# Softmax maxima of an attention stage turned by the DMA engines through DRAM, in place of TensorE and ScalarE

## The chip, the cores and the metric

The kernel runs on one core of one Trainium2 chip. The metric is the device time of one execution in microseconds. Before the change the median of three runs is 2610.9 us (2610.55 to 2611.96).

## The reference

A gated layer for 8 batches: `x` and `ctx` are 8 x 512 x 1024 (channels by positions). It normalizes `x` over its last axis, attends to `ctx` with 16 heads of 32 channels, adds the result times a gate, normalizes again, and adds a product with a 1024 x 1024 matrix whose operands are rounded to 8-bit floats, again gated.

```python
q = Wq @ layernorm(x) + bq; k = Wk @ ctx + bk; v = Wv @ ctx + bv      # per batch, 16 heads of 32 rows
dot  = einsum('bhdt,bhds->bhts', q, k) / sqrt(32)
mask = target_mask[:, :, :, None] * source_mask[:, :, None, :]
dot  = mask * dot - (1.0 - mask) * 1e6
amap = softmax(dot, axis=-1) * mask
x = x + tanh(g_xattn) * einsum('bhts,bhds->bhdt', amap, v)
x = x + tanh(g_ffn) * (f8(scale * layernorm(x)) / scale) @ (f8(scale1 * W2) / scale1)
```

## The kernel before

There are three stages. Setup turns the weights. The projections (to about 570 us) write q, k and v to DRAM scratch. The attention stage is where the change lies.

It works through 32 quads, a quad being four heads of one batch, in periods of 64 slots. TensorE issues all work in one written order (`period(n, p)` of the tensor block). In slot k of period n it issues one score matmul of quad n (`scores`, line 690): keys on the partitions, 512 queries in the columns, slots 0 to 31 for the query half th=0 and 32 to 63 for th=1. Beside it stands one matmul of the same scores the other way round, queries on the partitions (`scores_for_max`, line 703), 19 slots ahead of the quad's own period by `XLEAD` and `maxima_at`. VectorE takes each one's maximum along the row (line 849). Every fourth slot P·V follows (`times_v`, line 716), every eighth the sums of the probabilities (`denominators`, line 727), and at slots 34, 35, 50 and 51 the last product for quad n - 2 (`ffn`, line 742).

The softmax needs the maximum subtracted, and the score matmul does it: its operands have 100 rows, 96 for the products and two for the mask, and rows 98 and 99 of the stacked queries `q_st` hold the negated maximum of each query, in two parts (`KX, KS = 98, 100`). The maxima come out of VectorE with queries on the partitions, as `neg_max`, 128 x 32. They must become two rows of 16 x 128. Before the change that is done so: at slots 23 (th=1 of quad n) and 55 (th=0 of quad n+1) TensorE turns `neg_max` by a matmul with the identity (`turn_max`, line 734) into one of the three `x_bank` banks, ScalarE copies it out (`copy_max`, line 803), and SP writes it to `q_st` by one DMA (`set_max`, line 1035). `scores` waits for that DMA at slots 0 and 32 (`max_set`).

VectorE negates at slots 19 and 51 (`negate_max`, lines 858 to 865). The table `JOBS` deals the three banks to maxima, ffn halves and the two turns in order; `freed` says what each user waits for.

SP issues nearly all DMAs of the stage in one written order, and a wait of one holds all behind it. Around the two places: `turn_y8` (line 1031, a DMA transpose), `move_inv` (1011) and `spread_inv` (1017), which carry the inverse sums to DRAM and back for GpSimd's multiplication (line 951), `load_tm`, `load_v`, `move_den` (1007), the store of the output (`store`, 1044), and at the start of a period `stack` (990 to 996), the next quad's operands.

## Time and profile before

| | |
|---|---|
| median of 3 runs | 2610.9 us |
| the profiled execution's own time | 2608.16 us |
| its span | 2606.3 us |
| TensorE busy | 2505.3 us, 96% |
| VectorE busy | 1978.2 us, 76% |
| GpSimd busy | 1653.4 us, 63% |
| ScalarE busy | 1393.0 us, 53% |
| DMA | 242040 packets, 314.48 MB |
| matmuls of line 734 (the turn) | 64, median 298 ns |
| copies of line 803 | 64, median 266 ns |

The engine shares are over the whole span. The attention stage is a row of equal periods of some 61 us, so one period, cut out by windows and read in a timeline, stands for 30 others. Where a time is given without "us after", it is microseconds from the span's start.

### The profile page before, as it was taken

The numbers are of one execution on the slowest core, as the hardware profiler recorded it, in microseconds if no ns is written. First come the engines' busy times: TensorE is split into PE (matmuls) and PEld (weight loads), VectorE is DVE, ScalarE is ACT, GpSimd is POOL, SyncE is SP. The second block draws the span as 40 slices with busy tenths as digits, with TensorE's granted clock in tenths as the row PEclk, the third lists the DMA queues.
The fourth block names the chain that finished last, engine by engine and source line by source line (L and its number), as shares of the span: only waits on it lengthen the run. The fifth ranks groups of instructions, "written<-read, shape, count | busy, mean of one in ns | idle before, by whom it ended". The sixth has DMA issues, their size and how long they took to land.

```text
span 2606.3 us, 40566 instructions
## 1 busy us (share of the span) xinstructions
PE 2505.3 (96%) x13169; PEld 1385.0 (53%) x13169; DVE 1978.2 (76%) x3251; ACT 1393.0 (53%) x2606; POOL 1653.4 (63%) x1265
## 2 busy tenths in 40 slices
PE   5999999978999999999999999999999999999995
PEld 4888888864444444444444444444444444444441
DVE  5766666637788888888888888888888888888863
ACT  2333333322666666666666666666666666666662
POOL 1333333422777777777777777777777777777774
PEclk8999999996999999999999999999999999999997
DMA  6666666655334444444444444344444444444411
GB/s 213 229 236 236 234 234 233 237 171 96 76 80 89 88 96 91 98 103 99 103 98 93 91 93 93 88 88 88 96 91 96 102 100 102 100 94 92 91 37 49
DMA packets 242040, 314.48 MB, mean 121 GB/s; under 512 B 75033, under 2 KB 142681, under 8 KB 241857
## 3 DMA queue, kind: packets, MB, share of 16 engines
q1 hardware_dynamic: 229712, 274.20, 42.2%
q10 hardware_dynamic: 12144, 38.02, 4.1%
q8 instruction: 93, 1.52, 0.3%
q14 instruction: 91, 0.74, 0.1%
HBM read 200.09 MB, written 102.11 MB: 116 GB/s over the span
## 4 chain that ended last, share of the span: by engine, by line
PE 66%; DVE 6%; issue 3%; POOL 1%; DMA 1%; ACT 0%; SPq 0%; DVEq 0%; POOLq 0%; ACTq 0%
PE s_bank L690 19%; PE o_bank L716 18%; PE x_bank L703 16%; PE d_bank L727 7%; PE x_bank L742 5%; DVE part_max L849 4%; POOL pair_sum L942 1%; PE x_bank L734 1%; DVE y L103 1%; DMA q_st<-qx_scr 0%; DVE isnan L102 0%; POOL y L951 0%; ACT probs L785 0%; DMA inv_b<-inv_scr 0%; DVE neg_max L863 0%
## 5 line engine op out<-in xcount | busy, mean ns | idle before, releaser
L942 POOL TENSOR_TENSOR pair_sum<-probs 128x512 f32<-128x512 f32 x1024 | 1284.2, 1288 | 472.0 <-ACT probs L785 472.0
L849 DVE TENSOR_REDUCE part_max<-x_bank 128x1 f32<-128x512 f32 x2048 | 1280.9, 683 | 355.6 <-PE x_bank L703 348.8
L785 ACT ACTIVATE probs<-s_bank 128x512 f32<-128x512 f32 x2048 | 1071.5, 604 | 662.3 <-PE s_bank L690 655.0
L690 PE MATMUL s_bank<-q_st,k_st 100*128 100x512 f32 x2048 | 876.5, 430 | 4.7 <-ACT probs L785 4.7
L703 PE MATMUL x_bank<-k_st,q_st 98*128 98x512 f32 x2048 | 823.6, 406 | 24.8 <-DMA q_st<-qx_scr 21.5
L690 PEld LDWEIGHTS s_bank<-q_st,k_st 100*128 100x128 f32 x2048 | 387.1, 189 | 511.5 <-issue 263.2
L716 PE MATMUL o_bank<-probs,v_t 128*32 128x512 f32 x4096 | 545.5, 605 | 0.0
L703 PEld LDWEIGHTS x_bank<-k_st,q_st 98*128 98x128 f32 x2048 | 393.1, 192 | 141.8 <-DMA q_st<-qx_scr 22.0
L727 PE MATMUL d_bank<-pair_sum,ones 128*32 128x512 f32 x2048 | 266.6, 592 | 2.8 <-POOL pair_sum L942 2.8
L322 POOL TENSOR_TENSOR stage_lo<-stage,stage_hi 128x512 fp32r<-128x512 f32 x128 | 187.3, 1487 | 120.7 <-ACT stage_hi L392 120.1
L392 ACT ACTIVATE stage_hi<-stage 128x512 fp32r<-128x512 f32 x128 | 79.8, 632 | 190.2 <-DVE stage L476 142.9
L310 POOL TENSOR_TENSOR rstd<-ve,neg_half 128x4 f32<-128x4 f32 x8 | 14.6, 1830 | 251.8 <-DVE ve L507 251.8
L742 PE MATMUL x_bank<-w2q,y_t 128*128 128x512 bf16 x512 | 136.4, 393 | 26.3 <-DMA y_t<-y 23.5
L716 PEld LDWEIGHTS o_bank<-probs,v_t 128*32 128x32 f32 x4096 | 80.6, 108 | 143.4 <-issue 74.2
L727 PEld LDWEIGHTS d_bank<-pair_sum,ones 128*32 128x32 f32 x2048 | 66.5, 110 | 156.3 <-issue 152.0
L448 PE MATMUL bank<-c_hi,w_hi_k 128*128 128x512 f32 x256 | 100.6, 393 | 13.1 <-DVE c_lo L459 13.1
L409 ACT ACTIVATE stage<-stage,sm_now 128x512 f32<-128x512 f32 x64 | 45.4, 722 | 122.9 <-DVE stage L472 122.2
L472 DVE TENSOR_TENSOR stage<-bank,bias_v 128x512 f32<-128x512 f32 x64 | 43.5, 690 | 84.9 <-PE bank L448 84.3
L448 PE MATMUL bank<-c_lo,w_hi_k 128*128 128x512 f32 x256 | 101.8, 398 | 0.0
L448 PE MATMUL bank<-c_hi,w_lo_k 128*128 128x512 f32 x256 | 101.3, 396 | 0.0
L448 PE MATMUL bank<-w_hi_v,c_hi 128*128 128x512 f32 x256 | 101.3, 396 | 0.0
L448 PE MATMUL bank<-w_hi_v,c_lo 128*128 128x512 f32 x256 | 101.2, 396 | 0.0
(96 smaller groups left out, 2018.9 us busy)
## 6 DMA issues: line engine op xcount, KB each, us to landing
k_st<-k_scr SPq DMA_DIRECT2D x96, 512.0 KB
q_st<-q_scr SPq DMA_DIRECT2D x192, 256.0 KB
c_raw<-in_ctx_dram ACTq DMA_DIRECT2D x32, 512.0 KB, 6.7
x_raw<-in_x_dram ACTq DMA_DIRECT2D x32, 512.0 KB, 6.2
k_scr<-stage_hi SPq DMA_DIRECT2D x64, 256.0 KB, 2.4
k_scr<-stage_lo SPq DMA_DIRECT2D x64, 256.0 KB, 2.6
v_scr<-stage SPq DMA_DIRECT2D x64, 256.0 KB, 2.7
q_scr<-stage_hi SPq DMA_DIRECT2D x64, 256.0 KB, 2.1
```

The lines of the kernel that those rows point to most:

```text
L322: nc.gpsimd.tensor_tensor(stage_lo[:, e % STG], stage[:, g % STG], stage_hi[:, e % STG].bitcast(F32), ALU.subtract).then_inc(qk_lo, 1)
L392: nc.scalar.activation(stage_hi[:, e % STG], stage[:, g % STG], ACT.Copy).then_inc(qk_hi, 1)
L409: nc.scalar.activation(stage[:, g % STG], stage[:, g % STG], ACT.Copy, scale=sm_now[:, j:j + 1]).then_inc(v_masked, 1)
L448: last = nc.tensor.matmul(acc, a, m, start=(cb == 0 and n == 0), stop=(cb == CB - 1 and n == 2))
L690: nc.tensor.matmul(s_bank_of(n, k)[:, :], k_st[p][0:KS, h, j * P:(j + 1) * P], q_st[p][0:KS, th, h, :], start=True, stop=True).then_inc(sc ...
L703: nc.tensor.matmul(x_bank_of(n, "tile", k)[:, :], q_st[p][0:KX, th, h, tc * P:(tc + 1) * P], k_st[p][0:KX, h, sh * HALF:(sh + 1) * HALF], ...
L716: last = nc.tensor.matmul(o_bank[D * h:D * (h + 1), :], v_t[p][:, j, D * h:D * (h + 1)], probs[:, c % PR, h, :], start=(j == 0), stop=(j = ...
L727: last = nc.tensor.matmul(d_bank[D * h:D * (h + 1), :], ones[:, :], pair_sum[:, r % 2, h, :], start=(i == 0), stop=(i == 3))
L742: last = nc.tensor.matmul(x_bank_of(n, f"ffn{half}", k)[:, :], y8_t[:, kc, :], w2q[:, kc, half * HALF:(half + 1) * HALF], start=(kc == 0), ...
L785: nc.scalar.activation(probs[:, c % PR, h, :], s_bank_of(n, k)[:, :], ACT.Exp).then_inc(exp_done, 1)
L849: nc.vector.tensor_reduce(part_max[:, th, sh, at:at + 1], x_bank_of(n, "tile", k)[:, :], AX, ALU.max).then_inc(max_done, 2)
L942: nc.gpsimd.tensor_tensor(pair_sum[:, r % 2, h], probs[:, a, h], probs[:, a + 1, h], ALU.add).then_inc(pair_done, 1)
```

## The change

`neg_max` shrinks to the 32 columns that are used. Each time, SP stores it to DRAM as it lies (128 rows of 32 floats), waits for that store, and reads it back by two DMAs, one for each of the rows 98 and 99, whose source pattern takes elements 32 apart: 16 x 128 = 2048 elements of 4 bytes each. The turn, the copy, their semaphores and their two entries in the bank table go. The store and reads are issued ahead of `move_inv`, where the one DMA before stood behind it. `scores` now waits for both reads.

```diff
+    max_scr = nc.dram_tensor("max_scr", [TH, P, 2 * QH * TC], F32, kind="Internal").ap()
-            neg_max = sb("neg_max", [P, P], F32R, at)
-            max_rows = sb("max_rows", [2 * QH * TC, P], F32R, at)
+            neg_max = sb("neg_max", [P, 2 * QH * TC], F32R, at)
-            F_JOBS = {23: "max1", 34: "ffn0", 50: "ffn1", 55: "max0"}
+            F_JOBS = {34: "ffn0", 50: "ffn1"}
...
-                            pe.wait_ge(max_set, 16 * (2 * n + th + 1))
+                            pe.wait_ge(max_set, 32 * (2 * n + th + 1))
...
-                    def turn_max(n, k, m, th):
-                        pe.wait_ge(negmax_done, 3 * (2 * m + th + 1))
-                        wait_bank(n, f"max{th}", k)
-                        nc.tensor.matmul(x_bank_of(n, f"max{th}", k)[:, 0:P], neg_max[:, :], ident_r[:, :], start=True,
-                                         stop=True).then_inc(max_turned, 1)
...
-                    def copy_max(n, m, th, k):
...
-                        nc.scalar.activation(max_rows[:, :], x_bank_of(n, f"max{th}", k)[0:2 * QH * TC, 0:P],
-                                             ACT.Copy).then_inc(max_copied, 1)
...
+                    def store_max(m, th):
+                        sp.wait_ge(negmax_done, 3 * (2 * m + th + 1))
+                        if counted(32 * (2 * (m - 1) + th + 1)):
+                            sp.wait_ge(max_set, 32 * (2 * (m - 1) + th + 1))
+                        sp.dma_start(max_scr[th], neg_max[:, :].bitcast(F32)).then_inc(max_stored, 16)
+
                     def set_max(m, th, p):
-                        sp.wait_ge(max_copied, 2 * m + th + 1)
-                        sp.dma_start(q_st[p][KX:KS, th, :, :].bitcast(F32), max_rows[:, :].bitcast(F32)).then_inc(max_set, 16)
+                        sp.wait_ge(max_stored, 16 * (2 * m + th + 1))
+                        for part in range(2):
+                            rows = max_scr[th, :, part * QH * TC:(part + 1) * QH * TC].rearrange("t r -> r t").unsqueeze(0)
+                            sp.dma_start(q_st[p][KX + part:KX + part + 1, th, :, :].bitcast(F32).rearrange("o h (c t) -> o (h c) t", t=P),
+                                         rows, allow_slow_non_contiguous=True).then_inc(max_set, 16)
...
                             turn_y8(n - 2)
+                        if real(n):
+                            store_max(n, 1)
+                            set_max(n, 1, p)
                         if real(n - 1):
                             move_inv(n - 1, 1)
-                        if real(n):
-                            set_max(n, 1, p)
...
                             store(n - 2, p)
+                        if real(n + 1):
+                            store_max(n + 1, 0)
+                            set_max(n + 1, 0, 1 - p)
                         if real(n):
                             move_inv(n, 0)
-                        if real(n + 1):
-                            set_max(n + 1, 0, 1 - p)
```

On TensorE, around slot 23 of a period, before (`x_bank` are the banks for maxima, `neg_max` the negated maxima):

```order
L690 MATMUL s_bank<-q_st,k_st 128x512 [waits exp_done]
L703 MATMUL x_bank<-k_st,q_st 128x512 [waits max_done]
L734 MATMUL x_bank<-ident_r,neg_max 128x128 [waits max_done,negmax_done]
L716 MATMUL o_bank<-probs,v_t 32x512 [waits exp_done]
L716 MATMUL o_bank<-probs,v_t 32x512 x3
```

and in the changed kernel:

```order
L686 MATMUL s_bank<-q_st,k_st 128x512 [waits exp_done]
L699 MATMUL x_bank<-k_st,q_st 128x512 [waits max_done]
L712 MATMUL o_bank<-probs,v_t 32x512 [waits exp_done]
L712 MATMUL o_bank<-probs,v_t 32x512 x3
L686 MATMUL s_bank<-q_st,k_st 128x512 [waits exp_done]
```

The turn and its two waits are gone; all else keeps its order, and line numbers are 4 less.

On SP, from the load of the residual rows to the spread of the inverses (th=1), before:

```order
L1040 DMA res<-in_x_dram 128x1024 [waits out_stored]
L1031 DMA_TRANSPOSE y_t<-y 128x8x128 [waits ffn_done,norm_done]
L1011 DMA inv_scr<-inv_c 128x16 [waits inv_done]
L1035 DMA q_st<-max_rows 2x16x128 [waits max_copied]
L1017 DMA inv_b<-inv_scr 128x1x512 [waits norm_done,inv_moved]
```

and in the changed kernel:

```order
L1022 DMA res<-in_x_dram 128x1024 [waits out_stored]
L1004 DMA_TRANSPOSE y_t<-y 128x8x128 [waits ffn_done,norm_done]
L1010 DMA max_scr<-neg_max 128x32 [waits max_set,negmax_done]
L1016 DMA q_st<-max_scr 1x2048x1 [waits max_stored]
L1016 DMA q_st<-max_scr 1x2048x1
L984 DMA inv_scr<-inv_c 128x16 [waits inv_done]
L990 DMA inv_b<-inv_scr 128x1x512 [waits norm_done,inv_moved]
```

One DMA became three, the second waits for the first to land, and `move_inv` now stands behind them.

## Rows read from the trace of the kernel before

**Rows 1.** Windows: columns, and one steady period.
```profile
core 0: us, PE busy (x) PEld busy (x) DVE busy (x) ACT busy (x) POOL busy (x), PEclk, DMA share, GB/s
1400.00:1461.00 61.00, 60.70 (x340) 29.31 (x339) 50.40 (x87) 37.63 (x74) 45.24 (x35) 1.00 0.43 95
```

**Rows 2.** TensorE's timeline (start, us), slots 23 to 32.
```profile
1429.48 0.40 PE L703 MATMUL x_bank<-k_st,q_st 98*128 98x512 f32 x1
1430.04 0.30 PE L734 MATMUL x_bank<-ident_r,neg_max 128*128 128x128 f32 x1 [0.16 <-DVE part_max L849]
1430.27 1.06 PE L716 MATMUL o_bank<-probs,v_t 128*32 128x512 f32 x8
...
1433.01 0.40 PE L703 MATMUL x_bank<-k_st,q_st 98*128 98x512 f32 x1
1433.34 1.07 PE L716 MATMUL o_bank<-probs,v_t 128*32 128x512 f32 x8
...
1438.25 0.50 PE L690 MATMUL s_bank<-q_st,k_st 100*128 100x512 f32 x1
```

**Rows 3.** Timelines of VectorE and the SP queue, the same place.
```profile
1427.45 0.17 DVE L865 SCALAR_TENSOR_TENSOR neg_max<-row_max,neg_max 128x16 fp32r<-128x16 f32 x1
...
1428.72 1.27 SPq L1031 DMA_TRANSPOSE y_t<-y  x1
```

**Rows 4.** TensorE's timeline, slot 55, and slot 0 of the next period.
```profile
1461.73 0.40 PE L703 MATMUL x_bank<-k_st,q_st 98*128 98x512 f32 x1
...
1462.50 1.06 PE L716 MATMUL o_bank<-probs,v_t 128*32 128x512 f32 x8
...
1470.78 0.50 PE L690 MATMUL s_bank<-q_st,k_st 100*128 100x512 f32 x1
```

**Rows 5.** The SP queue's timeline there.
```profile
1460.07 0.35 SPq L1044 DMA_DIRECT2D out_dram<-res  x1
...
1469.66 1.30 SPq L990 DMA_DIRECT2D k_st<-k_scr  x3
```

**Rows 6.** DMA issues: count, KB each, median us from issue to landing.
```profile
out_dram<-res SPq DMA_DIRECT2D x32, 512.0 KB, 2.6
...
inv_scr<-inv_c SPq DMA_DIRECT2D x64, 8.0 KB, 1.4
...
y_t<-y SPq DMA_TRANSPOSE x32, 3.2
...
bias_k<-in_L_xattn_bk_dram ACTq DMA_DIRECT2D x1, 2.0 KB, 2.3
bias_q<-in_L_xattn_bq_dram ACTq DMA_DIRECT2D x1, 2.0 KB, 3.2
```

**Rows 7.** Windows: DMA share and GB/s stand last.
```profile
1.90:2.30 0.40, 0.00 (x0) 0.00 (x0) 0.11 (x1) 0.00 (x0) 0.00 (x0) 1.00 0.37 3
...
1427.00:1428.00 1.00, 1.00 (x9) 0.27 (x2) 0.90 (x6) 0.00 (x0) 0.12 (x1) 1.00 0.55 89
...
1430.00:1431.00 1.00, 0.96 (x9) 0.34 (x9) 1.00 (x2) 0.64 (x2) 1.00 (x2) 1.00 1.13 213
...
1461.00:1462.00 1.00, 1.00 (x5) 0.57 (x3) 1.00 (x2) 1.00 (x3) 0.65 (x1) 1.00 1.00 401
...
1465.40:1466.00 0.60, 0.57 (x6) 0.32 (x9) 0.60 (x2) 0.60 (x2) 0.60 (x1) 1.00 0.14 36
```

**Rows 8.** The ACT queue's timeline at the start of the program.
```profile
0.74 0.49 ACTq L174 DMA_DIRECT2D bias_k<-in_L_xattn_bk_dram  x1
...
1.27 0.52 ACTq L175 DMA_DIRECT2D bias_q<-in_L_xattn_bq_dram  x1
```

**Rows 9.** GpSimd's timeline, after slot 32.
```profile
1441.51 2.37 POOL L951 TENSOR_TENSOR y<-o_raw,inv_b 128x1024 f32<-128x1024 f32 x1
```

**Rows 10.** Windows: the granted clock early and late; and a wait of TensorE's.
```profile
623.50:628.50 5.00, 5.00 (x13) 3.94 (x13) 4.41 (x7) 2.81 (x5) 0.00 (x0) 0.50 1.04 208
628.50:633.00 4.50, 4.50 (x22) 2.54 (x21) 3.71 (x6) 3.20 (x7) 4.25 (x4) 0.96 1.05 165
...
2535.00:2540.00 5.00, 3.48 (x28) 1.09 (x20) 0.57 (x1) 2.09 (x5) 4.92 (x3) 1.00 0.00 0
...
2539.05 0.50 PE L690 MATMUL s_bank<-q_st,k_st 100*128 100x512 f32 x1 [1.52 <-ACT probs L785]
```

More of the change, by code:

```diff
@@ L584, in flamingo_gated_layer @@
             d_bank = pb("d_bank", [P, HALF], F32, at)
-            init_done = sem("init_done", at)
             stacked = [sem(f"stacked{i}", at) for i in range(TH)]
@@ L591, in flamingo_gated_layer @@
             negmax_done = sem("negmax_done", at)
-            max_turned = sem("max_turned", at)
-            max_copied = sem("max_copied", at)
+            max_stored = sem("max_stored", at)
             max_set = sem("max_set", at)
@@ L650, in quad_of_job @@
                     return maxima_at(n, k)[0]
-                return {"ffn0": n - 2, "ffn1": n - 2, "max1": n, "max0": n + 1}[kind]
+                return n - 2
             def freed(n, kind, k):
@@ L667, in freed @@
                         return max_done, 2 * NSLOT * m + 2 * (maxima_at(0, slot)[2] + 1)
-                    if was in ("ffn0", "ffn1"):
-                        return ffn_added, 2 * m + (was == "ffn1") + 1
-                    return max_copied, 2 * m + (was == "max1") + 1
+                    return ffn_added, 2 * m + (was == "ffn1") + 1
             def tile_of_max(i):
@@ L754, in period @@
                                 scores_for_max(n, k, m, (p + odd) % 2, i)
-                            if k == 23 and real(n):
-                                turn_max(n, k, n, 1)
-                            if k == 55 and real(n + 1):
-                                turn_max(n, k, n + 1, 0)
                             for half, at_ in ((0, 34), (1, 50)):
@@ L824, in period @@
                                 copy_den(n - 1, 1)
-                            if k == 23 and real(n):
-                                copy_max(n, n, 1, 23)
                             if k == 35 and real(n):
@@ L834, in period @@
                                 normalize(n - 1, 1 - p)
-                            if k == 55 and real(n + 1):
-                                copy_max(n, n + 1, 0, 55)
                     run(period)
@@ L854, in negate_max @@
                         dve.wait_ge(max_done, 2 * NSLOT * m + 2 * 32 * (th + 1))
-                        dve.wait_ge(init_done, 1)
                         if counted(done):
@@ L859, in negate_max @@
                         dve.wait_ge(negmax_done, done + 1)
-                        if counted(2 * m + th):
-                            dve.wait_ge(max_turned, 2 * m + th)
+                        if counted(16 * (2 * m + th)):
+                            dve.wait_ge(max_stored, 16 * (2 * m + th))
                         R = QH * TC
@@ L968, in period @@
                                 nc.gpsimd.tensor_tensor(rs2[:, :], ve2[:, :], neg_half[:, 0:1], ALU.pow).then_inc(rs2_done, 1)
-                    nc.gpsimd.memset(neg_max[:, :].bitcast(F32), 0.0).then_inc(init_done, 1)
                     run(period)
```

3 lines of the change are left out of this document (removed).

## The prediction

> **What bounds the kernel now.** The page comes first: by its engine shares TensorE alone is busy nearly throughout. One steady period of the attention stage, cut out by windows, says it without the average over stages [rows 1]. The reader is to see that TensorE works 60.70 of 61.00 us at full clock, with VectorE at 50.40, GpSimd at 45.24, ScalarE at 37.63. So each microsecond taken out of TensorE's row is worth a microsecond, if nothing else becomes late, and each microsecond in which TensorE waits is lost: there is no slack on it to catch up with. The attention stage has 32 such periods of 61.2 us; the change acts twice in each, 64 times in all. The rest of the reading is a race inside the period, from timelines of TensorE [rows 2, 4] and of VectorE and the SP queue [rows 3, 5]: when are the negated maxima ready, and when does the first score matmul need them?
>
> **What goes.** The turn on TensorE (line 734) goes, 64 times. Where it stands, the last score-for-maxima matmul starts at 1429.48, the turn itself at 1430.04 and the P·V matmuls at 1430.27: 0.79 us from first to last. Where there is none, the same two neighbours are 0.33 us apart (1433.01 to 1433.34) [rows 2]. In the other half period it is 1461.73 to 1462.50, 0.77 us [rows 4]. So a turn costs TensorE 0.45 us, of which only 0.30 are the matmul; the rest is the wait for its bank. 64 x 0.45 = 29 us less. ScalarE's copy is off the path, since ScalarE idles over a third of the period [rows 1]; I count it at nothing. The GpSimd memset is one instruction ahead of the stage: nothing.
>
> **What comes, and the race.** The new path is: VectorE finishes, SP issues a store of 16 KB, waits until it has landed, issues two reads of 2048 elements of 4 bytes each, and TensorE's first score matmul of that half waits for both. Behind that matmul in TensorE's row stand all others, those for the next quad's maxima too, so the wait stops everything.
>
> Half th=1. VectorE is done at 1427.6, but SP stands at the turning of y8, whose issue runs 1428.72 to 1429.99 [rows 3]. The store is issued at 1430.03. Its packets queue in the same rings behind the y8 transpose, which still moves 213 GB/s in 1430 to 1431 [rows 7] and lands 3.2 us after issue [rows 6], at 1431.9. A small store, the inverses, lands 1.4 us after issue [rows 6]; behind the transpose I take 2.0: 1432.05. SP then issues the first read at 1432.1. The first 4-byte packets of the bias load show 1.16 us after its issue at 0.74 [rows 7, 8], so data flow from 1433.26. After X us for all 4096 elements, and 0.55 more for the semaphore and TensorE's start (the bias load: 512 elements at 0.75 per ns end at 2.58, landing at 3.04 [rows 6, 8], and 0.1 for the start), the matmul can begin at 1433.81 + X. TensorE wants it at 1438.25 [rows 2], less the 0.45 gained by then: 1437.80. The stall is X - 4.0 us.
>
> Half th=0. SP stores the output at 1460.07 first [rows 5]; that lands after 2.6 us [rows 6], at 1462.67, with the rings full at 401 GB/s meanwhile [rows 7]. The maxima's store lands behind it, at about 1463.05; first read issued 1463.1; data from 1464.26; TensorE can begin at 1464.81 + X and wants to at 1470.78 - 0.45 = 1470.33 [rows 4]. The stall is X - 5.5 us.
>
> **The price X.** Nothing in this trace reads thousands of 4-byte elements, so I bound it. The only such transfers are the two bias loads at the start, 512 elements each, spread over 128 partitions. Window 1.90 to 2.30 holds nothing but them: 3 GB/s, which is 0.75 elements per ns [rows 7], so 4096 take 5.5 us. The busy share there is 0.37: if the rings could be filled, the same packets would pass in 5.5 x 0.37 = 2.0 us, the lower end. The upper end of the nearest rows: bias_q lands at 1.27 + 3.2 = 4.5, bias_k at 3.04 [rows 6, 8], 1.43 us for 512 elements, so 11.4 us for 4096. The new reads differ in one way that can only cost: all their elements go into one partition. The rows have a neighbour for that: the old write of 16 KB into two partitions, 36 GB/s at best in 1465.4 to 1466.0, where a transfer over all partitions reaches 401 [rows 7]. I take 5.5 plus a tenth: X = 6.0.
>
> The Trainium skill ("VectorE: DVE Perf Modes", in its trap on strided DMA copies, and "DMA: Bandwidth & Descriptors", Rules for kernel authors) says that a plain copy which transposes by its access pattern is 19 times slower than the hardware transpose. Taken at its word with the row of that transpose here (213 GB/s), 16 KB would take 0.077 x 19 = 1.5 us, and the change would be wholly hidden; the bias loads at 3 GB/s are 70 times slower, so I trust the row.
>
> **The sum.** Against the profiled execution's own 2608.2 us (span 2606.3; the median of the runs is 2610.9, 2.7 higher): turns -29; stalls 32 x (6.0 - 4.0) = +64 and 32 x (6.0 - 5.5) = +16. Together +51: 2659 us, 2662 on the median's scale; I give 2660.
>
> **What moves behind.** The inverses' store and spread stand behind the reads on SP and in the rings. In th=1 they feed GpSimd's multiplication at 1441.51 [rows 9]: reads end at 1439.3, the store of inverses lands some 0.5 later, the spread is issued at 1439.8 and lands near 1441.8, when GpSimd, itself shifted by the 2.0 us stall, comes at 1443.5. Hidden. In th=0 the loads of the next quad's stacks (issued 1469.66 before [rows 5]) wait for the spread: reads end 1470.3, stacks at 1471.4, about 1.2 us later against a TensorE that is itself 0.5 late and early by 0.45 a turn. Their first half (2.36 of 3.07 MB) must be in by slot 19, some 15.9 us after slot 0; the whole keeps the rings busy until 1427.5 in the period that began 61.1 us before 1470.78, at 1409.7 [rows 4, 7], so the half is there after 13 to 14 us. Hidden too, with 2 us to spare; if that cover went, up to 1 us per period, 32 us.
>
> **Rivals.** (a) *Hidden reads.* If X is under 4.75, the stall of th=1 is under 0.75 us and th=0 has none, so the turns win; at X of 4.0 or less the time is 2608 - 29 = 2579. For it: packets are busy for only 0.37 of the window, and the skill's rule of 19. Against it: the measured pace is 5.5 us, in rings nearly empty. Chance 0.18. (b) *One partition is a bottleneck.* Writes of 4 bytes into one partition serialise well below the pace of the bias loads. At X = 9.6 the stalls are 5.6 and 4.1: 179 + 131 - 29 = +281, 2889; at 11.4 they are 7.4 and 5.9: +397, 3005. For it: 36 against 401 GB/s. Against it: that row is of 512-byte packets, where bytes can be the limit. Chance 0.25. (c) *The clock falls.* The attention stage begins after a long wait for its first loads at a granted clock of 0.50, and only full work brought it back: 13 matmuls in 5.0 us, then 22 in 4.5 [rows 10]. That is 1.2 GHz of 2.4. If each of 64 stalls cost such a stretch, 5.0 us would do the work of 2.7, 2.3 us lost each, 147 in all: 2807. Against it: 1.52 us of waiting in 2535 to 2540 (3.48 of 5.00 busy) left the clock at 1.00 [rows 10], and my stalls are 2.0 and 0.5. Alone 0.05, within (b) likely, which then ends near 3030. (d) *Few engines.* Were the reads run on one DMA engine because the target is one partition, 4096 elements would take 16 x 5.5 = 88 us and the time would pass 7000 us. The old write into two partitions ran above the 25 GB/s that is one engine's share of 401, so several worked. Chance 0.02. The skill ("DMA: Bandwidth & Descriptors", on how many engines a DMA uses) takes the largest number up to 16 that divides the slowest dimension of both sides, here 16 and 2048, so 16 engines.
>
> **How the numbers follow.** My forecast, X between 5.05 and 8, has 0.43, and runs from 2613 to 2787. A band of X from 4.75 to 5.05 ends within 0.2% of before (5 us, what a measurement of this kernel can tell from none): 0.07. (a) 0.18, (b) 0.25, (c) 0.05, (d) 0.02. Faster 0.18, same 0.07, slower 0.75. The range goes from 2577, all hidden, to 2950, X near 10.5: it leaves out (d) and the worst of (b).
>
> **What would show it.** TensorE's waits after: the first score matmul of each half (a line that now waits for nothing) should head them, released by the read of max_scr, 32 times near 2.0 us and 32 times near 0.5; the th=1 wait the longer one. The read issues should follow the store's by 2.0 and 2.6 us. In windows, GB/s while only the reads flow should be near 2.7. P·V matmuls should follow 0.33 us after the last maxima matmul. I am wrong if the reads' window is as short as 4 us or as long as 9, if the wait of th=0 is the longer, if the clock shows 0.50 inside periods, or if another wait (the stacks, the inverses) stands beside that on the maxima.

## The result, and the profile of the changed kernel

The changed kernel takes 3989.1 us (median of 4 runs, 3975.4 to 4002.8) against 2611.4 us (2610.6 to 2612.6) for the one before on the same chip: ratio 1.5275, 95% interval 1.5217 to 1.5333. The forecast was 2660, with a range to 2950. The profiled execution took 3975.4 us, span 3973.6.

| | before | after | difference |
|---|---|---|---|
| span, us | 2606.3 | 3973.6 | +1367.3 |
| TensorE busy | 2505.3 | 2707.9 | +202.6 |
| TensorE idle (span less busy) | 101.0 | 1265.7 | +1164.7 |
| waits of TensorE on the maxima's read | none | 1060.3 | +1060.3 |
| waits of TensorE on the stacks (the first load's alone is 21.5) | 21.5 | 137.9 | +116.4 |

TensorE's idle time has two new heads. The groups of instructions by line, of the changed kernel (busy us, mean ns of one | idle time ahead of them and what ended it):

```profile
L686 PE MATMUL s_bank<-q_st,k_st 100*128 100x512 f32 x2048 | 948.1, 465 | 1063.9 <-DMA q_st<-max_scr 1060.3 <-ACT probs L771 3.6
L699 PE MATMUL x_bank<-k_st,q_st 98*128 98x512 f32 x2048 | 890.6, 439 | 142.8 <-DMA q_st<-qx_scr 137.9 <-DVE part_max L824 4.9
```

Before, the same two groups had 876.5 us (430 ns) and 823.6 us (406 ns) of busy time, and 4.7 and 24.8 us of idle time. The list of waits gives the number of times: 64, one for each half of a block, 16.6 us on average (548 us in the 32 of th=0, 512 in the 32 of th=1).

```profile
PE s_bank L686 <- DMA q_st<-max_scr: 1060.3, 64, 21.0
POOL y L925 <- DMA inv_b<-inv_scr: 569.3, 32, 22.6
```

One block, as windows give it, answers to [rows 1]: it is 106 us long instead of 61, with TensorE busy for 69.42, at a mean granted clock of 0.77.

```profile
2006.89:2113.26 106.37, 69.42 (x337) 32.35 (x337) 51.53 (x86) 37.75 (x71) 45.19 (x35) 0.77 0.58 54
```

TensorE's timeline answers to [rows 2, 4]. The P·V matmuls now follow the last matmul for the maxima after 0.33 us, as where no turn stands; the first score matmul of each half waits 14.52 and 18.98 us, and it and its successors take 0.80 and 0.63 us instead of 0.50 and 0.40:

```profile
2016.70 0.40 PE L699 MATMUL x_bank<-k_st,q_st 98*128 98x512 f32 x1
2017.03 1.06 PE L712 MATMUL o_bank<-probs,v_t 128*32 128x512 f32 x8
2032.61 0.80 PE L686 MATMUL s_bank<-q_st,k_st 100*128 100x512 f32 x1 [14.52 <-DMA q_st<-max_scr]
2033.20 0.63 PE L699 MATMUL x_bank<-k_st,q_st 98*128 98x512 f32 x1
...
2086.32 0.80 PE L686 MATMUL s_bank<-q_st,k_st 100*128 100x512 f32 x1 [18.98 <-DMA q_st<-max_scr]
```

The SP queue in the same block answers to [rows 3, 5]. The reads' issue follows the store's by 1.91 and 2.39 us; the spread of the inverses and the next stacks come only after the reads have landed, and now right behind one another, 0.67 us apart. Before, the spread stood 4.3 us ahead of the stacks' issue at 1469.66 [rows 5]:

```profile
1465.36 0.55 SPq L1017 DMA_DIRECT2D inv_b<-inv_scr  x1
```

And in the changed kernel:

```profile
2005.48 1.31 SPq L1004 DMA_TRANSPOSE y_t<-y  x1
2006.89 0.52 SPq L1010 DMA_DIRECT2D max_scr<-neg_max  x1
2008.80 1.90 SPq L1016 DMA_DIRECT2D q_st<-max_scr  x2
2012.06 0.80 SPq L984 DMA_DIRECT2D inv_scr<-inv_c  x1
2032.74 0.60 SPq L990 DMA_DIRECT2D inv_b<-inv_scr  x1
...
2057.71 0.37 SPq L1010 DMA_DIRECT2D max_scr<-neg_max  x1
2060.10 1.87 SPq L1016 DMA_DIRECT2D q_st<-max_scr  x2
2062.02 9.89 SPq L984 DMA_DIRECT2D inv_scr<-inv_c  x1
2086.46 0.58 SPq L990 DMA_DIRECT2D inv_b<-inv_scr  x1
2087.13 1.37 SPq L963 DMA_DIRECT2D k_st<-k_scr  x3
```

The DMA issues (last number: median us from issue to landing) answer to [rows 6]: the inverses' store, 1.4 before, sits behind the reads.

```profile
q_st<-max_scr SPq DMA_DIRECT2D x128, 8.0 KB, 22.6
max_scr<-neg_max SPq DMA_DIRECT2D x64, 16.0 KB, 2.0
inv_scr<-inv_c SPq DMA_DIRECT2D x64, 8.0 KB, 22.2
```

The windows of that read answer to [rows 7, 10] (clock, DMA share and GB/s last). This is the strangest picture of the trace: the recorded packets are over soon after 2020, some eleven microseconds after the reads were issued; then the DMA engines show nothing for twelve microseconds, and only then, at 2032.6, does the read land. In that silence the granted clock falls to 0.50 (1.2 of 2.4 GHz).

```profile
2009.00:2012.00 3.00, 3.00 (x18) 1.45 (x16) 2.96 (x6) 1.86 (x4) 3.00 (x4) 1.00 0.83 3
...
2018.00:2020.00 2.00, 0.09 (x4) 0.00 (x0) 0.28 (x1) 0.00 (x0) 2.00 (x2) 1.00 1.61 4
2020.00:2024.00 4.00, 0.00 (x0) 0.00 (x0) 0.00 (x0) 0.00 (x0) 1.27 (x2) 0.74 0.02 0
2024.00:2028.00 4.00, 0.00 (x0) 0.00 (x0) 0.00 (x0) 0.00 (x0) 0.00 (x0) 0.50 0.00 0
...
2034.00:2038.00 4.00, 4.00 (x11) 1.90 (x10) 2.01 (x3) 1.58 (x4) 0.42 (x1) 0.50 0.18 66
2042.00:2060.00 18.00, 18.00 (x103) 8.49 (x101) 15.26 (x28) 12.42 (x24) 12.39 (x12) 1.00 0.09 33
```

### The profile page after: what moved, and what is told of

It reads as the page before. It is cut to its first block, busy times and chain, and to the rows that moved or that the text cites. A ratio compares the mean times of both kernels' runs of the same rounds, so it can differ in the third digit from the quotient of the medians.

```text
span 3973.6 us, 40435 instructions
## 1 busy us (share of the span) xinstructions
PE 2707.9 (68%) x13105; PEld 1463.1 (37%) x13105; DVE 2005.0 (50%) x3251; ACT 1399.1 (35%) x2542; POOL 1651.4 (42%) x1264
## 4 chain that ended last, share of the span: by engine, by line
DMA 55%; PE 19%; SPq 5%; DVE 3%; issue 2%; POOL 1%; ACT 0%; DVEq 0%; POOLq 0%; ACTq 0%
DMA q_st<-max_scr 36%; DMA q_st<-qx_scr 14%; PE s_bank L686 6%; PE x_bank L699 5%; PE o_bank L712 3%; DMA max_scr<-neg_max 3%; PE x_bank L732 3%; DMA inv_scr<-inv_c 2%; PE d_bank L723 1%; SPq L967 1%; SPq L1016 1%; SPq L1004 1%; SPq L963 1%; DVE row_max L832 1%; DVE part_max L824 1%
## 5 line engine op out<-in xcount | busy, mean ns | idle before, releaser
L686 PE MATMUL s_bank<-q_st,k_st 100*128 100x512 f32 x2048 | 948.1, 465 | 1063.9 <-DMA q_st<-max_scr 1060.3
L686 PEld LDWEIGHTS s_bank<-q_st,k_st 100*128 100x128 f32 x2048 | 425.0, 208 | 1614.4 <-DMA q_st<-max_scr 1118.0
L699 PE MATMUL x_bank<-k_st,q_st 98*128 98x512 f32 x2048 | 890.6, 439 | 142.8 <-DMA q_st<-qx_scr 137.9
L712 PE MATMUL o_bank<-probs,v_t 128*32 128x512 f32 x4096 | 587.2, 647 | 0.0
L699 PEld LDWEIGHTS x_bank<-k_st,q_st 98*128 98x128 f32 x2048 | 432.9, 212 | 274.9 <-DMA q_st<-qx_scr 151.3
L925 POOL TENSOR_TENSOR y<-o_raw,inv_b 128x1024 f32<-128x1024 f32 x32 | 75.7, 2364 | 569.3 <-DMA inv_b<-inv_scr 569.3
L723 PE MATMUL d_bank<-pair_sum,ones 128*32 128x512 f32 x2048 | 294.9, 650 | 2.7 <-POOL pair_sum L916 2.7
L732 PE MATMUL x_bank<-w2q,y_t 128*128 128x512 bf16 x512 | 165.5, 458 | 23.0 <-DMA y_t<-y 22.9
L449 PE MATMUL bank<-x_hi,w_lo_q 128*128 128x512 f32 x256 | 101.3, 396 | 0.0
L449 PE MATMUL bank<-w_lo_v,c_hi 128*128 128x512 f32 x256 | 101.1, 395 | 0.0
```

The lines of the kernel that those rows point to most:

```text
L449: last = nc.tensor.matmul(acc, a, m, start=(cb == 0 and n == 0), stop=(cb == CB - 1 and n == 2))
L686: nc.tensor.matmul(s_bank_of(n, k)[:, :], k_st[p][0:KS, h, j * P:(j + 1) * P], q_st[p][0:KS, th, h, :], start=True, stop=True).then_inc(sc ...
L699: nc.tensor.matmul(x_bank_of(n, "tile", k)[:, :], q_st[p][0:KX, th, h, tc * P:(tc + 1) * P], k_st[p][0:KX, h, sh * HALF:(sh + 1) * HALF], ...
L712: last = nc.tensor.matmul(o_bank[D * h:D * (h + 1), :], v_t[p][:, j, D * h:D * (h + 1)], probs[:, c % PR, h, :], start=(j == 0), stop=(j = ...
L723: last = nc.tensor.matmul(d_bank[D * h:D * (h + 1), :], ones[:, :], pair_sum[:, r % 2, h, :], start=(i == 0), stop=(i == 3))
L732: last = nc.tensor.matmul(x_bank_of(n, f"ffn{half}", k)[:, :], y8_t[:, kc, :], w2q[:, kc, half * HALF:(half + 1) * HALF], start=(kc == 0), ...
```

## The experiments

### What a transfer of small elements costs by itself (m1_transfers, m2_transfers)

Both programs hold transfers alone and leave the whole computation out. Each transfer stands alone on the chip, three times; VectorE waits for it and makes a mark. The basic one is the kernel's own read of half its rows:

```
q.dma_start(one_row[98:99, ...], scr.rearrange("t r -> r t") ...)      # 2048 x 4 B
```

> This kernel leaves out all computation: it only makes single transfers, three times each, one after another, each followed by a small VectorE copy that waits for it. Theory (writes): a 4-byte write into SBUF costs about 5.6 ns at the place where all the engines' writes meet (4096 in 22.8 us), and it counts where they meet. So 2048 elements into partition 98 land after about 12 us, 1024 after about 6.5, the pair into 98 and 99 after about 23, and the pair into 98 and 70 distinctly sooner than 23; 2048 elements into 16, 32 or 128 partitions land in under 5 us, since the writes fan out; sources 8 bytes apart in place of 128 change nothing for partition 98 (12 us); 16-byte elements, 2048 of them, take about the same 12 us; 64 packets of 512 bytes take about 3 us. Rival (reads): strided 4-byte reads of DRAM are the limit. Then 16, 32 and 128 partitions take as long as one (12, 23, 12 us), the pair into 98 and 70 as long as the pair into 98 and 99, and sources 8 bytes apart are faster than 128. Rival (partial lines): writes into the same line of SBUF wait for each other; then targets 32 bytes apart in partition 98 land much sooner than adjacent ones. The transposing store into DRAM has no forecast from either; I guess 3 to 6 us.

> Again no computation, single transfers three times each. One partition took 12.7 us for 2048 elements of 4 bytes, 16 neighbouring partitions 3.4. Theory A, writes into one partition pass one after another at some 5.5 ns: then the same 2048 into partition 98 issued so that only 4 DMA engines take part still land after 12 to 13 us; into four neighbouring partitions (96 to 99) and into four partitions 4 apart (96, 100, 104, 108) with 4 engines both land alike, in some 11 us if the 4 engines themselves become the limit (21 ns each) or 4 to 5 us if not. Theory B, 16 engines disturb each other in one place: then 4 engines into one partition are faster than 16. Theory C, the port that four neighbouring partitions share is the limit: then 96 to 99 take as long as one partition (12.5) and 96, 100, 104, 108 about a quarter. 16 partitions 8 apart: as 16 neighbours, 3.4 us. 1024 packets of 64 bytes into one partition: about 6.5 us, if it is the number of writes that counts. The transposing store into 8 KB of DRAM took 11 to 12.5 us; with targets 512 bytes apart over 1 MB it lands much sooner if the narrow region is the cause, alike if each small write into DRAM is.

VectorE's timeline of the first program; the idle time in brackets is the transfer, from issue to landing. In this order: one partition, 2048 elements; 1024; two partitions (98 and 99), 4096; 16 partitions, 2048; 32 partitions, 4096; one partition with its targets 32 bytes apart; 2048 pieces of 16 bytes; 64 pieces of 512 bytes (one of each three shown):

```profile
45.54 0.15 DVE L113 COPY mark<-src 128x1 f32<-128x1 f32 x1 [12.76 <-DMA one_row<-scr]
...
60.20 0.15 DVE L113 COPY mark<-src 128x1 f32<-128x1 f32 x1 [6.77 <-DMA one_row<-scr]
...
118.20 0.15 DVE L113 COPY mark<-src 128x1 f32<-128x1 f32 x1 [25.03 <-DMA one_row<-scr]
...
221.85 0.15 DVE L113 COPY mark<-src 128x1 f32<-128x1 f32 x1 [3.41 <-DMA many_rows<-scr]
...
240.09 0.15 DVE L113 COPY mark<-src 128x1 f32<-128x1 f32 x1 [4.05 <-DMA many_rows<-scr]
...
280.12 0.15 DVE L113 COPY mark<-src 128x1 f32<-128x1 f32 x1 [10.33 <-DMA wide_row<-scr]
...
343.85 0.15 DVE L113 COPY mark<-src 128x1 f32<-128x1 f32 x1 [11.19 <-DMA wide_row<-scr]
...
371.78 0.15 DVE L113 COPY mark<-src 128x1 f32<-128x1 f32 x1 [2.85 <-DMA wide_row<-scr]
```

And of the second: one partition, written with an outer dimension of four so that four DMA engines should carry it; four neighbouring partitions (96 to 99) from four engines; four partitions 4 apart from four engines; 1024 pieces of 64 bytes into one partition; a store of 2048 elements into 8 KB of DRAM; the same with its targets 512 bytes apart over 1 MB:

```profile
73.93 0.15 DVE L138 COPY mark<-src 128x1 f32<-128x1 f32 x1 [12.90 <-DMA one_row<-scr]
...
105.30 0.15 DVE L138 COPY mark<-src 128x1 f32<-128x1 f32 x1 [9.00 <-DMA one_row<-scr]
...
124.76 0.15 DVE L138 COPY mark<-src 128x1 f32<-128x1 f32 x1 [4.93 <-DMA one_row<-scr]
...
158.81 0.15 DVE L138 COPY mark<-src 128x1 f32<-128x1 f32 x1 [6.07 <-DMA wide_row<-scr]
...
193.47 0.15 DVE L138 COPY mark<-src 128x1 f32<-128x1 f32 x1 [11.36 <-DMA turned<-src]
...
202.28 0.15 DVE L138 COPY mark<-src 128x1 f32<-128x1 f32 x1 [4.21 <-DMA big_rows<-src]
```

What follows: the reading side is not the limit, since the same number of elements out of the same kind of source goes into 16 partitions in 3.4 us and into one in 12.8; nor does a source whose elements lie 8 bytes apart in place of 128 help (13.5 us into one partition). Into one partition 2048 elements cost some 6 us more than 1024 (12.8 less 6.8 to 7.0), and 4096 into two some 12 more than 2048: 5.8 and 6.0 ns each. It is a price per write, not per byte: 4, 16 and, with half as many pieces, 64 bytes cost about the same each. Targets 32 bytes apart take 10.3 to 11.2 us, so writes that disturb each other at adjacent addresses explain about a fifth. The kernel's 4096 elements into two partitions take 25.0 us here; in the block above 23.8 and 26.2 us pass from the first read's issue to the waiting matmul. A narrow stretch of DRAM behaves alike, 11.4 against 4.2 us (10.7 to 12.6 in the first program).

By its packets, the transfer meant for four engines did not run on four. The number of its packets tells it, against the one into four neighbouring partitions (DMA view of the second program, windows 61.00 to 73.90 and 87.00 to 96.10):

```profile
DMA packets 2064, 0.01 MB, mean 1 GB/s; under 512 B 2064, under 2 KB 2064, under 8 KB 2064
...
DMA packets 2052, 0.01 MB, mean 1 GB/s; under 512 B 2052, under 2 KB 2052, under 8 KB 2052
```

2048 are the elements. What is over is 16 in the first, as in the basic transfer, and 4 in the second; the 1024 elements have 8 over. The trace does not name these packets, but the updates of the semaphore rise with them (16, 5 and 9), so I read them as one for each engine that takes part. The three repeats (12.8 to 14.1 us) are then more runs on sixteen engines, and what fewer engines would do with one partition was not tried, apart from the 1024 elements on eight, at nearly the price of sixteen.

Neighbours in a group of four get in each other's way, on four engines both times: 9.0 against 4.9 us. The Trainium skill ("SBUF — State Buffer", Door 1: The DMA port swizzle) lets four such neighbours share a DMA port, and puts partitions 4 apart on different ports; the trace agrees with that. Why one partition is slower still (12.9) stays open, since that ran on sixteen engines and these on four.

### The turning alone taken out (e1_contiguous)

The same store, the same two reads into the same two partitions, but in runs as the memory has them: rows 98 and 99 get unturned values.

```
-rows = max_scr[th, :, part * QH * TC:...].rearrange("t r -> r t")
+rows = max_scr[th, part * HALF // 8:..., :].rearrange("a (b r) -> (a b r)", r=32)...
```

> The maxima go through DRAM as in the changed kernel but are read back in runs of 512 bytes, so rows 98 and 99 hold unturned values (the turning is left out). If the 4-byte elements alone are the cost: reads land 2 to 2.5 us after issue, no wait of TensorE on them, the granted clock back at 0.98, and the gain of the removed turns shows whole: about 2582 us (29 less than before). If the hop through DRAM (store, wait, read) were a cost of its own, about 1 to 2 us of waiting per half would stay: 2610 to 2700 us.

Measured: 2582.1 us (2578.1 to 2584.0), ratio 0.9888 [0.9871, 0.9904], with no wait of TensorE on the maxima. Everything that the change adds except the small elements (the store, its landing, two issues, SP standing meanwhile) is hidden, and the removed turns give back some 29 us, the -29 of the forecast. The whole loss comes from elements of 4 bytes, by themselves or by what they hold up.

### Half of the elements (e2_half)

Row 98 is read element by element, row 99 in runs (unturned). Edit: as above, under `if part == 1`.

> Only row 98 is read back element by element; row 99 is read in runs of 512 bytes (the low parts of the maxima are unturned). Theory (each 4-byte write costs about 5.6 ns): landing after about 12.5 us instead of 22 to 25, waits of TensorE about 5.5 us at slot 32 and 7.5 at slot 0 where the changed kernel has 14.5 and 19.0, so near 3000 to 3150 us with the clock still falling. If the cost were a fixed one per transfer or came from the backlog of two transfers, the time would be near that of the changed kernel (above 3700) or near before (below 2750).

Measured, one run: 3272.0 us, above the 3000 to 3150 expected. TensorE's waits on the maxima fall from 1060.3 to 378.9 us:

```profile
PE s_bank L686 <- DMA q_st<-max_scr: 378.9, 64, 10.3
```

That is 10.6 us less per half for 2048 elements less, 5.2 ns each; the time falls by 703 us, of which these waits are 681. A fixed cost per transfer is out.

### The inverses ahead of the maxima on SP (e3_inverses_first)

```
+    move_inv(n - 1, 1); spread_inv(n - 1, 1)
     store_max(n, 1); set_max(n, 1, p)
-    move_inv(n - 1, 1); spread_inv(n - 1, 1)      (th=0 alike)
```

> The store and spread of the inverses are issued ahead of the store and reads of the maxima; nothing is left out. Theory: of the 1378 us lost, the waits on the next quad's stacks (118 us) come only because the inverses' completion stands behind the reads. They should go, and with them the clock loss there: TensorE's wait on the stacks falls below 30 us. But the reads start some 4 us later, after the inverses, which lengthens each wait on them by about 3 to 4 us (some 220 us). Sum: within 150 us of the changed kernel, rather slower. If the reads' landing were set by other traffic behind them, landing would change from 22 to 25 us; I expect it not to.

Measured, one run: 4312.0 us, 323 above the changed kernel where at most 150 was expected. The stacks' issue no longer waits for the reads to land, and TensorE's wait on them is back at 22.0 us, the first load's alone; but the reads start later, also because the store, now 0.7 us behind the spread of the inverses, lands after 4.4 to 4.6 us instead of 1.9 to 2.4 (medians), and the waits on the maxima grow to 1595.2 us. The read itself lands as late after its issue as before (chain of waits):

```profile
2037.18 23.01 DMA q_st<-max_scr
```

So the 116 us on the stacks come from what stands behind the reads' landing, and moving it costs more than it gives.

### Does the clock's fall cost the 200 us? (e5_busy_wait, e8_no_idle)

Both put matmuls whose result nobody reads ahead of slots 0 and 32 of the changed kernel; the computation stays.

```
+ if k in (0, 32) and real(n) and real(m):
+     for _ in range(FILL): nc.tensor.matmul(x_bank_of(n, "tile", k)[:, :], ident_b[:, :], w2q[:, 0, 0:HALF], ...)
```

FILL is 56 in the first, 78 and 70 in the second.

> The changed kernel, and before the score matmul of slots 0 and 32 TensorE runs 56 more matmuls (bfloat16, 512 columns, about 12 us) whose results are overwritten unread. They fill most of the wait on the reads (14.5 and 19.0 us). If the fall of the granted clock costs what TensorE's busy time shows (2708 against 2505 less 19 for the turns, 222 us), the time falls by 130 to 220 us, to 3770 to 3860, and the clock at the restart is 1.00 at slot 32. If the clock were not what the rest of the loss is, the time would stay at 3990 or rise.

> The changed kernel with unused matmuls ahead of slots 0 and 32 as in the kernel with 56 of them, now 78 and 70 (17.1 and 15.3 us at full speed), so that they reach past the landing of the maxima; they leave the computation as it is. In the kernel with 56, TensorE idled 2.85 and 4.38 us ahead of each restart and ran at the lower clock for some 5 us behind it. Theory (the lower clock after each wait costs the changed kernel some 200 us): no idle rest, no fall, each restart at 1.00; 5 us at half speed are 2.5 us of lost work, 64 times: 160 to 220 us less than the 3975 us of the kernel with 56, so 3755 to 3815 us. Rival (the DMA's landing sets the period whatever TensorE's clock): within 0.5% of 3975. Third: the matmuls overshoot the landing by 0 to 1 us each and eat part of it: 3800 to 3880 us.

Measured: 3975.2 us, ratio 1.5239 [1.5187, 1.5291], and 3986.0 us, 1.5277 [1.5248, 1.5305]. Both expectations were missed. In the block shown the first kernel still rests 2.85 us ahead of slot 32 and restarts at the lower clock; in the second the restart runs at full pace. TensorE's timeline, first kernel, then second:

```profile
2031.52 0.80 PE L687 MATMUL s_bank<-q_st,k_st 100*128 100x512 f32 x1 [2.85 <-DMA q_st<-max_scr]
```

```profile
2035.66 0.50 PE L687 MATMUL s_bank<-q_st,k_st 100*128 100x512 f32 x1 [0.95 <-DMA q_st<-max_scr]
```

So the first kernel tests little: its own work took 2692.9 us (busy 3466.3 less 773.4 of filler), 15 less than in the changed kernel. In the second it shrank from 2707.9 to 2596.1 us (busy 3598.5 less 1002.4), which is half of the 222 us that lie above the full clock. The list of its waits says where these 112 us went:

```profile
PE x_bank L700 <- DMA q_st<-qx_scr: 191.4, 31, 22.0
PE s_bank L687 <- DMA q_st<-max_scr: 61.4, 35, 20.1
PE s_bank L687 <- ACT probs L776: 45.4, 37, 2.3
```

The waits on the stacks grew by 53 us, those on ScalarE by 42 (3.6 in the changed kernel, 4.7 before; ScalarE in its turn waited 129.5 us for GpSimd, which waits for the inverses). Both of these waits hang on SP, and SP hangs on the landing of the reads. My reading is that the period is paced by chains from one landing to the next: behind th=0, SP issues the stacks only at 2087, and they land 18.12 us after the last issue of their first half (2090.48), 17.4 in the second kernel (median). The lower clock is real and takes some 200 us of TensorE's time, but removing half of it gave nothing back. What the other half is worth was not tried.

### The elements spread over 32 partitions (e4_spread, e10_inv_between, e7_reordered)

The turned read goes into a tile of 32 partitions, as many as there are rows, and a third transfer of 512-byte runs puts them into the two rows.

```
-sp.dma_start(q_st[p][KX + part:...], max_scr turned)  x2
+sp.dma_start(max_rows[:, :], max_scr[th].rearrange("t r -> r t"))
+sp.wait_ge(max_spread, ...)
+sp.dma_start(q_st[p][KX:KS, th, :, :], max_rows[:, :])
```

> The same elements are read one by one, but into 32 partitions, and a second transfer carries those rows in runs of 512 bytes into the queries; nothing is left out. If the place where the writes meet is the cause, the reads land after about 4 us, the second transfer 2 us later: 8 us after the store's issue. Slot 32 then waits some 0.5 us, slot 0 not at all: 2608 - 29 + 16, about 2598 us, the clock at 0.98. If strided 4-byte reads were the cause, the landing would be above 12 us and the time above 3200.

Measured: 2829.4 us, ratio 1.0837 [1.0820, 1.0854]. The read landed as forecast, and TensorE waited 4.6 us in all for the maxima; a new wait replaced it. The chain and the list of waits:

```profile
1486.15 4.01 DMA max_rows<-max_scr
```

```profile
PE x_bank L701 <- DMA q_st<-qx_scr: 181.5, 31, 21.6
```

Three steps on SP instead of one (store 2.4, read 4.0, the transfer that sets 0.7) hold the stack's issue, 10.0 us behind the store instead of 8.4 in e1. But late issue is the smaller part. Worked out from the issues and completion signals of each trace (medians over the blocks): before, in e1 and in e6 the stack is issued 1.1 us ahead of slot 0, and its first half, for which slot 19 waits, lands 15.6 to 15.8 us later, 1.1 to 1.2 us before slot 19 wants it. In e4 it is issued 1.2 us later than that, and lands after 21.1 us, 5.3 longer; in the changed kernel 1.9 us later and after 21.4. What goes with the longer landing is the spread of the inverses (256 KB) right ahead of the stack in the same queue:

| kernel | from the spread's issue to the stack's | the stack's first half lands after |
|---|---|---|
| before, e1, e6 | 3.6 to 4.0 us | 15.6 to 15.8 us |
| e9 | 1.4 | 18.4 |
| e10 | 1.3 | 19.0 |
| e4, changed kernel | 0.7 | 21.1, 21.4 |
| e7 (spread behind the stack) | none near | 15.6 |

That the spread itself slows what follows it is my reading; no run moved it alone, but e10 below has a transfer on both sides of it. Each wait on the stacks also brings a stretch at the lower clock. Two kernels tried to win it back by SP's order. In e7 the first inverses go behind the stack, the second store of the maxima goes ahead of the y8 transpose, and in th=1 the store and the spread of the inverses go between the read and the transfer that sets:

> The maxima are stored and read element by element into 32 partitions (max_rows), and one transfer puts them into the stacked queries, as in the kernel that spread them; what is new is SyncE's order: the first inverses of a block go behind the next stack instead of ahead of it, the store of the second maxima ahead of the y8 transpose, and the second inverses' store between the read and the transfer that sets. Theory (the time is set by where small elements land and by who stands behind the wait on SyncE): the stack's issue is no longer held, the wait of 181.5 us in 31 pieces goes back to some 25, and TensorE's clock no longer falls once a period, which cost the rest of the 250 us: 2585 us (2575 to 2605), 0.99 of the kernel before. Rival (the stack's own transfer is slowed by the element-wise traffic that shares the rings with it): the landing stays at 17 to 18 us and PE waits 3 to 6 us per block: 2700 to 2830 us. Third: the inverses, now landing under the stack's transfer, arrive late and VectorE waits for inv_c's store: 2620 to 2680 us.

Measured: 2863.4 us, ratio 1.0965 [1.0939, 1.0991], a miss. The wait on the stacks is gone (21.8 us, the first load's). But the inverses' store now lies in the rings behind the stack, SP waits for it, and what comes after it slips; new are TensorE's waits for VectorE (90.7 us) and, at slot 32, for the maxima (84.4 us). The chain of waits has the store:

```profile
1444.83 14.65 DMA inv_scr<-inv_c
```

In e10 the inverses' store goes between the read and the transfer that sets, and in th=1 their spread too:

> The maxima are read element by element into 32 partitions, with SyncE's order of the first kernel that spread them (2829 us) changed in one respect: the inverses' store is issued between the element-wise read and the transfer that sets the rows, so that its landing (1.7 us) lies beside the read's (4.0 us) and SyncE reaches the stack 2.5 us sooner (8.0 instead of 10.5 us behind the maxima's store; the kernel with unturned rows has 8.4 us). Nothing goes behind the stack's 1.3 MB, where the reordered kernel's inverses took 14.7 us to land. Theory (what was left of the loss in the first was the stack's late issue, 181.5 us of waits, and the lower clock behind them): waits on the stacks back to 22 to 70 us, 2590 us (2580 to 2640). Rival (the 4096 small elements hold up the stack's own landing): waits stay at 150 to 180 us, 2780 to 2830 us.

Measured: 2821.2 us, ratio 1.0815 [1.0786, 1.0843], another miss. The stack's wait halves, though the stack is issued as early as before, and about the same amount appears at the maxima:

```profile
PE x_bank L701 <- DMA q_st<-qx_scr: 93.3, 31, 21.5
PE s_bank L688 <- DMA q_st<-max_rows: 84.3, 32, 7.4
```

The waits at the maxima are again those of slot 32 (all but one), where the transfer that sets stands 0.6 us behind the spread. It lands late there:

```profile
1452.39 4.68 DMA q_st<-max_rows
```

The medians are 4.7 us in th=1 of e10 and 4.8 in e7, but 2.3 in th=0 of both and in both halves of e4, where it is ahead of the spread. From the store (1445.13) to the first score matmul (1457.11) it makes 12.0 us, where the kernel before has some 8. So e7 and e10 share one fault, and an order that keeps the spread away from the stack and from the transfer that sets was not tried.

### The turn on VectorE (e6_vector_turn, e9_turn_later)

VectorE transposes the 128x32 tile by blocks of 32, and four transfers of 128-byte runs set the rows; no store and no wait on SP.

```
+nc.vector.transpose(neg_t[:, :], neg_max[:, :])
-store_max, set_max (two turned reads)
+for b in range(4): sp.dma_start(q_st rows, columns 32*b..., neg_t[32 * b:32 * b + 32, :])
```

> No DRAM and no TensorE: VectorE turns each 32 x 32 block of the negated maxima in place of the turn, and SP writes the four blocks into the queries by four transfers in runs of 128 bytes; nothing is left out. 512-byte packets into one partition land in 2.9 us for 64 of them; 128 packets of 128 bytes should take 128 x 5.5 = 0.7 us plus the start, so all land 4 us after the first issue, at 1434.5 where slot 32 wants them at 1437.8. VectorE has 10 us of slack per period for 2 x 0.2 us. The gain of the turns shows whole: 2582 us, as in e1. If the four issues on SP (1.8 us) delay the inverses or the stacks, up to 10 us of it is lost.

Measured: 2609.3 us, ratio 0.9992 [0.9983, 1.0001]: no change, where 2582 was expected. The maxima are in time, but the score-for-maxima tiles now wait for VectorE, 79.3 us in 139 pieces (TensorE and its weight loads together) instead of 22.6 in 55: behind its busiest stretch (slot 19) stands one more operation of 0.2 us and its semaphore, and inv_c took 1.40 us there instead of 0.36 in the block looked at, 0.85 on average against 0.41 in e1. TensorE's saved 0.45 us a half is given back. The second kernel moves the turn to slots 24 and 56, and the inverses' store ahead of the four transfers:

> The kernel in which VectorE turns the maxima by 32x32 blocks and four transfers of 128-byte runs set them, with the turn moved from right behind the negated maxima (slots 19 and 51) to slots 24 and 56, and the inverses' store ahead of the four transfers on SyncE. Theory (it lost the 27 us of the freed TensorE time because the turn lengthened VectorE's busiest stretch, and PE waited for part_max): the waits for VectorE fall from 79.3 us to about 23, and the time to 2585 us (2578 to 2595). Rival (VectorE has no slack in any slot; 64 turns of 0.21 us plus their waits come out as time wherever they stand): 2605 to 2615 us. Third: the maxima now land after slot 32 starts (four issues of 2.65 us and a landing of 2 us in 7.8 us): PE waits up to 1 us each, 2620 to 2670 us.

Measured: 2650.8 us, ratio 1.0151 [1.0136, 1.0165]. The first half of the theory held, TensorE's waits for VectorE in front of the maxima tiles fell from 21.2 to 3.9 us; but the four issues (2.66 us) and the spread now stand right ahead of the stack's, 1.4 us from spread to stack instead of 3.6. The stack is issued on time and its first half lands after 18.4 us instead of 15.6:

```profile
PE x_bank L698 <- DMA q_st<-qx_scr: 69.1, 30, 22.0
```

Of the kernels that leave nothing of the computation out, none was faster than the one before by more than 0.2%.

## Why the prediction was wrong

**The step that failed** is "The price X": 4096 elements in 6.0 us, with 11.4 as the upper end. From the trace after, by the forecast's own formula (1.16 from issue to first data, 0.55 from landing to start): 2032.61 - 2008.80 - 1.71 = 22.1 us in th=1, 2086.32 - 2060.10 - 1.71 = 24.5 in th=0; the median over all blocks is 22.5 in both. The pace was taken from the bias loads [rows 7], whose 512 elements go into 128 partitions. The forecast named the difference, called it one that "can only cost", and priced it at a tenth. It is a factor of nearly four: 12.8 us into one partition, 3.4 into sixteen (m1_transfers). Its upper end was no bound, since it came from rows in which the suspected limit could not show itself.

**The sum's other terms at that price.** With X at 22.1 and 24.5 the forecast's stalls are 18.1 and 19.0 us; measured 14.5 and 19.0 in the block shown. The th=0 one fits in this block. In th=1 TensorE comes 3.4 us later than reckoned (11.2 us from store to slot 32, not 7.8), because the slots there run at the lower clock behind a wait on the stacks. In this block that makes the th=0 wait the longer; over all blocks it is 17.1 us on average against 16.0. The forecast had named four signs of being wrong on this side, and all four came: a read far longer than 9 us, the longer wait in th=0, a clock of 0.50 inside the periods, and another wait, on the stacks.

**Rival (b)**, one partition as a bottleneck, 0.25, named the mechanism and fell far short in size (9.6 to 11.4). The row for it, 36 GB/s into two partitions [rows 7], was of 32 pieces of 512 bytes and showed no price per write. Rival (a) is out for one partition; into 32 partitions the same elements land in 4.0 us. Rival (d), one engine, is out by its own price, 88 us, and each read of the changed kernel has sixteen signals of completion, so the sixteen engines of the forecast came true.

**Rival (c)**, the clock, came with (b) as the forecast said it would: TensorE's busy time grew by 203 us while the turns took 19 away. But its price as an addition to the time is not borne out: e8 freed 112 us of TensorE's time and the time did not move.

**"Hidden too, with 2 us to spare"**, of the stacks, failed: the waits on them grew by 116 us, and e3 shows that they come from what stands behind the reads' landing. The forecast had the stacks issued 1.2 us late and the half there 13 to 14 us after slot 0. The first half was there 14.7 us after slot 0 before, with 1.1 us to spare and not 2, and 22.2 after the change: 1.9 for the late issue, the rest because it took 5.6 us longer to land, a term that the forecast put at nothing. (Its 3.07 MB are 3072 KB, so 3.15 MB beside the 2.36; that moves its 13 to 14 us by 0.3.) The inverses were called hidden as well; GpSimd waited 569 us for them, and in the changed kernel that cost TensorE next to nothing (3.6 us behind ScalarE); with the clock kept up in e8 it cost 45.

**What held:** the turns' 29 us (e1: ratio 0.9888, and the 0.33 us between the neighbours); the two distances from store to read, 1.91 and 2.39 us for 2.0 and 2.6; the store's landing hidden; the place and the number of the waits, 64, at the first score matmul of each half. The 2.7 GB/s forecast for the reads held only for their first 3 us (3, then 2 and 1 GB/s; the 4 at the end has the inverses' store in it).

The Trainium skill's factor of 19 for a turning copy ("VectorE: DVE Perf Modes", The three transpose paths), weighed in the forecast and set aside, would have made X 1.5 us, an estimate. The Trainium skill gives the factor there for a large innermost stride at the destination; here the destination is contiguous and the source strided. The measurement decides: 22.1 and 24.5 us, 15 times that. In these runs there is no fixed factor; it depends on how many partitions take the pieces (2048 into sixteen in 3.4 us, into one in 12.8).

**What stays open.** The profile records nothing between the engines' packets, over by 2020, and the landing at 2032; that it is the small writes which are still being done there is argued, from the price per write, and not shown. Nor was it tried whether two rows in different groups of four, read by different queues, do better; 98 with 70 took 23 to 25 us, like 98 with 99, but the two stood one behind the other in the same rings.

## What to carry to other kernels

Count a DMA's pieces by where they land: thousands of small writes into one partition, or into a few KB of DRAM, cost some 5 to 6 ns each here; over 16 partitions or more the same pieces landed in 3 to 4 us, but the second step that puts them in place has its own price (e4, 8%). When the trace has no row for the new operation's worst feature, the nearest row is no upper bound; say so, and widen the range by what that feature could do alone. And where a change puts a wait into a queue, price everything that is issued behind it, and ask what will then stand close together: here the stacks had 1.1 us of slack, and every order tried saved one wait and paid with another.

## What the hardware showed unexpectedly

- A transfer can land 12 us after its last recorded packet, and a later, small store in the same queue lands only with it: 22.2 us instead of 1.4. The landing, not the DMA share, is what to read.
- What was issued within 1.4 us behind the spread of the inverses landed 2.0 to 5.6 us later than elsewhere: the stack (18.4 to 21.4 us for 15.8), the store of the maxima in e3 (4.4 to 4.6 for 1.9 to 2.4), the transfer that sets (4.7 for 2.3).
- The length of a rest alone does not tell the clock of the restart. After 2.85 us (e5, 2031.52) TensorE ran at a granted clock of 0.50 for some 5 us, and so it did after 1.54 us in e8 (3607.58); it restarted at 1.00 after 3.22 us there (1932.86), as after 0.95 us and after the 1.52 of [rows 10].
- SP's issue of a store behind these reads took up to 9.89 us (2062.02), 2.0 us in the median, where 0.34 is usual in e1: the issue itself was held, with some 4100 small pieces issued just before.
- VectorE turned a 128x32 tile of 4-byte values by blocks of 32 in 0.20 us.
